# Both sum tensors of an expert layer used to its last expert and added in another order at the end; two moves in the stage before

## The reference, cut to what matters

```python
x = _layernorm(x + _L0_attn_ref(x, ...))      # linear attention, 16 heads, chunks of 128 tokens
x = _layernorm(x + _L0_xattn_ref(x, ids, ctx, ctx, ctx))  # each token goes to one of 4 experts, picked by its id
x = _layernorm(x + _L0_ffn_ref(x, ...))       # router over 128, 48 kept; 8 experts for each token

# in _L0_xattn_ref, for e in range(4):
g = silu(einsum('bsd,fd->bsf', h, Wg[e]));  u = einsum('bsd,fd->bsf', h, Wu[e])
y = einsum('bsf,df->bsd', g * u, Wd[e]);    out = where(expert_ids == e, y, out)

# in _L0_ffn_ref:
top_v, top_i = top_k(softmax(where(old_to_new == -1, -inf, x @ gate_weight.T)), 8)
gu = einsum('ech,eoh->eco', xb, gate_up_proj); h = silu(g) * u     # xb: at most 192 rows for each of 48 experts
out = einsum('eci,ehi->ech', h, down_proj)
final = zeros_like(x).at[tok].add(out_row * weight)                # what is summed at the end of the kernel
```

## Time and profile before

| | |
|---|---|
| median of three runs | 914.21 us |
| the profiled execution | 917.26 us |
| its span | 915.5 us |
| PE busy | 857.3 us (94%) |
| DVE, ACT, POOL busy | 650.0, 402.2, 465.5 us |
| mean granted clock of PE | 0.987 |
| DMA | 155.24 MB, 170 GB/s over the span |

### The profile page before, as it was taken

How to read it: one execution, slowest core, us unless ns; L and a number is a source line. 1 busy time by engine, 2 the same in 40 slices (tenths; PEclk the granted TensorE clock), 3 DMA queues, 4 the chain that set the end, 5 groups by cost and what they waited for, 6 DMA issues and landing times.

```text
span 915.5 us, 18727 instructions
## 1 busy us (share of the span) xinstructions
PE 857.3 (94%) x6020; PEld 722.9 (79%) x6021; DVE 650.0 (71%) x1475; ACT 402.2 (44%) x825; POOL 465.5 (51%) x441
## 2 busy tenths in 40 slices
PE   6899999999999978999999888999999999999985
PEld 4677777777777767888888677998998899888863
DVE  6856776567765774777777887767777677676876
ACT  4332333333333332332332145666666666666634
POOL 0332233433234241465555456776777777777454
PEclk9999999999999998999999899999999999999998
DMA  9461111211112017222322349999999999999975
GB/s 340 145 253 47 48 47 46 92 46 46 46 55 72 25 47 240 88 98 87 108 88 87 115 134 293 293 293 287 291 297 296 293 290 290 292 289 228 247 206 197
DMA packets 72430, 155.24 MB, mean 170 GB/s; under 512 B 9904, under 2 KB 10560, under 8 KB 72000
## 3 DMA queue, kind: packets, MB, share of 16 engines
q1 hardware_dynamic: 50240, 99.81, 33.7%
q0 software_dynamic: 22144, 54.85, 23.5%
HBM read 110.55 MB, written 44.07 MB: 169 GB/s over the span
## 4 chain that ended last, share of the span: by engine, by line
PE 68%; DVE 15%; issue 7%; ACT 4%; DMA 3%; POOL 1%; DVEq 0%; SPq 0%; ACTq 0%; POOLq 0%
PE ps L629 24%; PE ps L1029 18%; PE ps L1049 10%; PE ps L1018 3%; PE ps L734 2%; DVE arena L1514 2%; PE ps L724 2%; DVE arena L1453 1%; DMA xg<-x_rows,place_token 1%; DMA arena<-in_xT 1%; DVE arena L1447 1%; PE ps L810 1%; PE ps L895 1%; ACT o_hi L1267 1%; ACT arena L1119 1%
## 5 line engine op out<-in xcount | busy, mean ns | idle before, releaser
L2170 POOL DMA_INDIRECT y_rows<-arena,place_token x92 | 154.6, 1681 | 66.5 <-issue 48.3
L2159 POOL DMA_INDIRECT xg<-x_rows,place_token x96 | 94.4, 984 | 41.8 <-issue 27.1
L1029 PE MATMUL ps<-arena,raw 128*128 128x192 f32 x576 | 98.2, 327 | 1.4 <-DVE arena L1877 1.3
L1029 PEld LDWEIGHTS ps<-arena,raw 128*128 128x128 f32 x576 | 94.5, 190 | 4.8 <-issue 2.5
L629 PE MATMUL ps<-w_hi,x_hi 128*128 128x512 f32 (+1 forms) x324 | 76.1, 357 | 9.1 <-ACT arena L1119 4.7
L2025 POOL TENSOR_TENSOR arena<-arena,attn_pack 128x512 f32<-128x512 f32 x12 | 15.6, 1304 | 119.1 <-DVE arena L1465 119.1
L1029 PE MATMUL ps<-arena,mid_flat 128*128 128x192 f32 x432 | 73.2, 326 | 0.0
L629 PE MATMUL ps<-w_hi,x_lo 128*128 128x512 f32 (+1 forms) x324 | 73.2, 348 | 0.0
L1029 PEld LDWEIGHTS ps<-arena,mid_flat 128*128 128x128 f32 x432 | 71.0, 190 | 2.2 <-DVE arena L1877 0.3
L629 PE MATMUL ps<-w_lo,x_hi 128*128 128x512 f32 (+1 forms) x324 | 71.7, 343 | 0.0
L629 PEld LDWEIGHTS ps<-w_hi,x_hi 128*128 128x128 f32 x324 | 51.3, 189 | 21.1 <-issue 8.3
(11 more groups left out here) (281 smaller groups left out, 2067.1 us busy)
## 6 DMA issues: line engine op xcount, KB each, us to landing
raw<-in_gu SPq DMA_DIRECT2D x24, 768.0 KB
mid_flat<-in_gu SPq DMA_DIRECT2D x18, 768.0 KB
raw<-in_dn SPq DMA_DIRECT2D x24, 256.0 KB
y_rows<-zero SPq DMA_DIRECT2D x20, 256.0 KB
mid_flat<-in_dn SPq DMA_DIRECT2D x18, 256.0 KB
arena<-in_gu SPq DMA_DIRECT2D x6, 768.0 KB
arena<-in_xT SPq DMA_DIRECT2D x16, 256.0 KB
x_res<-in_x SPq DMA_DIRECT2D x16, 256.0 KB, 2.8
```

The lines of the kernel that those rows point to most:

```text
L1029: m = pe.matmul(out, wgu[slot][:, q, part * P:(part + 1) * P], xgT[:, p, q, :], start=(q == 0), stop=(q == KC - 1))
L2159: pool.indirect_dma_start(out=xg[:, place, h, :], out_offset=None, in_=x2_d, in_offset=bass.IndirectOffsetOnAxis(ap=place_token[:, 2 * n + ...
L2170: pool.indirect_dma_start(out=y2_d if p and n < DUAL else y_d, out_offset=bass.IndirectOffsetOnAxis(ap=place_token[:, 2 * n + h:2 * n + h ...
```

## The change

It has four parts. (1) `DUAL` is 46: all odd experts go to `y2_d`, and no scatter waits for its neighbour. (2) SP loads the even sums `y_d` into `y2_all` (four loads when expert 44 has landed, four between the others), and `y2_d` into `y_all` when expert 45 has. POOL adds the two, and is three pieces ahead; DVE takes the first tile of pieces 0 and 1; DVE adds PSUM for tiles 0 to 9; for tiles 10 to 15 (`SUMMED` = 10) PE adds the finished sum by one product with the unit matrix. (3) In stage two, PE's `route` stands behind the second `turn_h`. (4) `low_ctx(1)` and the following low parts are each moved one place ahead, and two matmuls that keep PE busy stand ahead of `first_up`.

```diff
-DUAL = 42
+DUAL = 46
-EARLY = 4
-SUMMED = NT - 4
+EARLY = 2
+SUMMED = NT - 6
...
+        def even_in(eng, lo, hi):
+            for q in range(lo // 2, (hi + 1) // 2):
+                eng.wait_ge(y2_in[q % 2], 16 * (q // 2 + 1))
...
-            sp.wait_ge(y_added[1], 32 * (DUAL // 2))
-            for q in range(NT // 2):
+            sp.wait_ge(y_added[0], 32 * (DUAL // 2))
+            def load_even(q):
                 at_least(sp, y2_in[q % 2], 16 * (q // 2))
...
+            for q in range(NT // 4):
+                load_even(q)
             sp.wait_ge(place_made, NG + 1)
+            sp.wait_ge(y_added[1], 32 * (DUAL // 2))
             for p in range(2):
-                sp.wait_ge(y_added[p], 32 * (E2 - KEPT) // 2)
...
-                sp.dma_start(y_all[:, slice(*PIECES[q]), :], rows_of(y_d, q)).then_inc(y_in[q % 3], 16)
+                sp.dma_start(y_all[:, slice(*PIECES[q]), :], rows_of(y2_d, q)).then_inc(y_in[q % 3], 16)
+                if 1 <= q <= NT // 4:
+                    load_even(NT // 4 + q - 1)
...
             def b_tile(j, p, k, left, place):
-                if is_later(j):
-                    route(p, k - 1)
                 turn_h(p, k, 0)
...
                 turn_h(p, k, 1)
+                if is_later(j):
+                    route(p, k - 1)
...
+            keep_warm(PS + 3, 2)
             first_up()
...
-            def sum_of_both(j):
...
-                pe.matmul(ps[:, KEPT_BANKS[j % 8], :], eye, y2_all[:, j, :], start=False, stop=False)
+            def add_sum(j):
+                pe.wait_ge(r3_too, j + 1 - EARLY)
                 pe.matmul(ps[:, KEPT_BANKS[j % 8], :], eye, y_all[:, j, :], start=False, stop=True).then_inc(kept_made, 1)
...
             first_slots()
+            low_ctx(1)
             dve.wait_ge(rms_made, t + 1)
...
-            low_ctx(1)
+            low_ctx(2)
...
-            low_ctx(2, (0,))
+            low_ctx(E1 - 1, (0,))
...
             low_x1(0, 0)
-            low_ctx(2, (1,))
-            low_ctx(E1 - 1)
+            low_ctx(E1 - 1, (1,))
...
+            for i in range(EARLY):
+                lo, hi = PIECES[i]
+                even_in(dve, lo, hi)
+                dve.wait_ge(y_in[i], 16)
+                dve.tensor_tensor(y_all[:, lo, :], y_all[:, lo, :], y2_all[:, lo, :], ALU.add).then_inc(r3_made, 1)
...
-            last_sum(0)
+            for q in range(3):
+                last_sum(q)
             for q, (lo, hi) in enumerate(PIECES):
-                if q + 1 < LAST and PIECES[q + 1][0] < SUMMED:
-                    last_sum(q + 1)
+                if q + 3 < LAST:
+                    last_sum(q + 3)
                 pool.wait_ge(ve_made, NT + SLOT_T + q + 1)
```

## The result

Four runs of the changed kernel took 918.72 to 921.61 us, median 919.95; four of the kernel before 913.24 to 916.01, median 914.50. The ratio is 1.0056, with a 95% interval of 1.0035 to 1.0077: slower, by 5.1 us (3.2 to 7.0). The forecast was 915.2, the range 909.0 to 919.0. The profiled execution took 921.61 (span 919.7), against 917.26 before.

The account below looks back on a forecast made before the run. PE was taken as the busiest engine, near its limit in the loops, with stretches where it stands or runs slowly. -2.3 - 2.6 + 5.2 + 0.7 = +1.0 on 914.21 gave 915.2 us, range 909.0 to 919.0.

Parts of the forecast that it names:

- Part one, the low weights: Start of stage two: two low halves leave ahead of the first `hidden`, which comes 2.3 us earlier; bounds -2.3 and 0.
- Part two, the clock: PE from 346 to 352 us: full clock in place of 0.50 saves 2.6 us; bounds -2.6 and 0.
- Part three, the ring: Stage two: `route`, `hidden`, register load, `turn_x` and product close a ring of 8.91 us against 8.585; sixteen rounds, +5.2.
- the upper bound: Stage two's rounds: if the residual sum's wait of 0.60 us stays inside the ring, up to +14.8; called unlikely.
- Part four, the tail: Last scatters to last statistics: loads begin 3.6 us earlier, but PE waits for POOL's sums; +0.7, bounds -2.8 and +3.7.
- my 894.7 for tile 10's sum: Tail: POOL finishes the first tile of pair 5 at 894.7 us, until when PE waits from 891.4.
- the rival with the clock: Tail: PE's clock falls behind its wait for tile 10, if piece 5 lands 0.5 us late; +3.0, 918.2, chance 0.12.
- the lower bound of -2.8: Tail: were PE fed in time, it would end at 903.5 us, 2.8 less than before.
- The two clocks: Rivals: clock falls at 346 all the same (917.8, chance 0.17); clock falls in the tail (918.2, chance 0.12).

Follow-up runs that it names:

- first_warm: `low_only` plus four matmuls behind `first_up` and three ahead of the first down product, in PE's waits; ratio 0.9966 to the kernel before.
- low_only: Kernel before with only the low weights moved ahead and the two matmuls ahead of `first_up`; ratio 0.9971, faster by 2.7 us (0.8 to 4.5).
- route_only: Kernel before with only PE's router product moved behind the second `turn_h`; ratio 1.0061, slower by 5.6 us (3.7 to 7.3).
- tail_only: Kernel before with only the sums' part of the change (`DUAL` 46, SP's loads, sums on all engines); ratio 1.0029, slower by 2.6 us (0.9 to 4.3).
- route_back: Changed kernel with the router's product put back ahead of `turn_h`; ratio 1.0010 to the kernel before.
- tail_warm: `route_back` plus twenty matmuls that nobody reads in PE's wait ahead of tile 10's sum; ratio 0.9973 to the kernel before.
- base_again: The same kernel as `first_warm`, run again on the last chip; ratio 0.9958 to the kernel before, 904.74 us against 908.53.

## Why the prediction was wrong

*Part one, the low weights, -2.3: right.* From `first_up`'s first product to `hidden` it was 6.03 us before (338.61 to 344.64) and 3.77 after (338.18 to 341.95): -2.26.

*Part two, the clock, -2.6: this step failed.* "I take -2.6, as the waits ahead of 346 are what sets this stretch apart from the rounds behind it". That much was right, since in `first_warm` the filled waits kept the clock; but I credited the change with it because one wait of 1.75 us went, and the waits of 1.07, 0.37 and 0.77 stayed. The clock fell all the same, at 345, for some 3.4 us instead of 6.8; tile 0's round went from 10.09 to 9.61. Up to tile 1's down product the profile gives -3.3 for parts one and two, so -1.1 of the -2.6; by the times `low_only` gives -2.7 for both, not -4.9.

*Part three, the ring, +5.2: right.* 8.91 us forecast, 8.82 to 8.85 measured, which is 3.7 to 4.3 us for sixteen rounds; +5.6 (3.7 to 7.3) by the time of `route_only`. Link by link in the round shown: `route` to the residual sum 4.07 (4.13), to the end of `hidden` 2.19 (2.17), to `turn_x` 0.81 (0.90), to the product 0.68 (0.71), to `route` 1.03 (1.00). The 0.60 that the residual sum had waited is gone, as I said of the upper bound.

*Part four, the tail, +0.7: this step failed too,* with +2.6 by `tail_only`. Stage three ended 0.9 earlier, so my 894.7 for tile 10's sum is 893.8 on this time; it came at 895.3. The first load went at 876.22 for 874.8 (the scatter began 0.8 behind its rows and took 0.5 longer to land), and landed 4.9 behind its issue and not 3.3. And I let POOL be paced by the landing of pieces 3, 4 and 5, when its own chain set the time: 2.99, 0.96 of waiting for an even load, 5.15, 0.73, 2.48, 0.70 and 1.24 from 881.12 on. The sum was 1.5 us late, and the rival with the clock had named 0.5. The clock fell: at half speed PE lost 2.9 us in this profile and 1.7 in `route_back`'s, and by the times `tail_warm` gains 3.4 (1.3 to 5.5) by keeping it. That is more than the 1.9 between my +0.7 and the +2.6. I had computed a wait of 3.3 us on PE, put its effect on the clock at nothing in the sum, and gave that rival 0.12.

The DVE side was mis-sized as well. I counted 0 for POOL and DVE shutting each other out; it was 4.5 us of DVE's time, hidden behind the slow PE in the changed kernel and the bound once PE was repaired. So the lower bound of -2.8, with PE fed in time, wasn't to be had either: `tail_warm` feeds it, and its tail is 2.1 longer than the old one. The Trainium skill's rule (SBUF — State Buffer, section Who interferes with whom) was weighed for the shifts and not for the two sums that the change gives to DVE and POOL at the same moment. The trace agrees with it there most of all: DVE's pair took 3.52 us, nearly the 1.3 of its own and the 2.5 of POOL's one behind the other.

*The sum.* -2.7 for parts one and two, +5.6 and +2.6 make +5.5, or 919.7 for 919.95. The two clocks were two rivals of mine (917.8 and 918.2), each taken with everything else as forecast. Both came true, so the time lay beyond the range. They weren't exclusive: both hang on waits of PE, which the old rows show or which I had computed, and which the change leaves or makes.

Not settled: the profiled executions of the changed tail are longer by 4 to 6 us and the times by 2.6. The stretch at half speed, which lasts 3.4 to 6.2 us, accounts for how the profiles differ, but the times have no such record of theirs. And with a clock of 1.00 the tail is still 2.1 us above the old one in the profile, where the ratios of `tail_warm` and `low_only` are 0.0002 apart, each uncertain by 0.0016 to 0.0020. In these two profiles stage three differs the other way (379.2 us for `tail_warm`, 381.2 for `low_only`); no run tells whether that is the change's doing or chance.

## What to carry to other kernels

Before a product is moved behind a wait on an in-order engine, follow who reads it, and add up the way from there back to that wait: if it closes, the sum of the links is the least period, and here it could be read from the old trace to 0.1 us. Where a forecast has PE stand for some microseconds ahead of dense matmuls, carry the half-speed stretch behind it in the sum, not in a rival; and here the clock was not mended by taking away one of four waits. When work is given to POOL beside DVE, add nearly the length of a POOL sum to each DVE sum or shift that reads all it needs from SBUF and meets one: here 1.1 us to each, whether it took 0.65 us alone or 0.15.

## What was new of the hardware

- In `first_warm`, seven matmuls of 256 columns in PE's waits of 1.1 and 0.8 us (and two ahead of `first_up`) kept the granted clock at 1.00 from 338 to 354, where it had fallen in the kernel before, in the changed one and in `low_only`.
- The same wait of about 4.5 us ahead of tile 10 was followed by 3.4 us at 0.50 in one profile and 5.9 in another.
- DVE and POOL, each with two sums of 128x512 from SBUF begun together, took 3.52 and 2.99 us; alone such pairs take 1.3 and 2.5. DVE's sums with one input from PSUM kept 1.3 us a pair beside the same POOL sums (880.92 in `tail_warm`, 1.28).
- Series on different chips differ by more than the changes here: the kernel before took medians of 915.7, 914.9, 916.5 and 908.5 in four series, each on another chip. In the last one the rounds of `base_again` were 8.38 us, where the same kernel (`first_warm`) had 8.55 in the second. Only ratios from one series can be compared closely.
